# Two engines' orders in a slot loop: VectorE searches a tile's masked scores one slot earlier, and ScalarE counts the older tile first

## The chip, the cores and the metric

The kernel runs on one core of a Trainium2 chip. The metric is the device time of the whole program in microseconds (us): the median of three runs before the change is 3109.65 us (3107.92 to 3110.01). Another kernel's time is compared with it on the same chip.

## What is computed

The reference, cut to what matters. x has 16 sequences of 512 rows of 256 numbers; there are 16 heads of 16 numbers.

```python
Q, K, V = (x @ W.T + b, split in heads)
scores = einsum('bhqd,bhkd->bhqk', Q, K) / sqrt(D)          # 512 x 512 for each of 16 x 16 heads
thresh = top_k(scores, 31).values[..., -1:]                 # the 31st largest of each row
scores = where(scores < thresh, -inf, scores)
context = softmax(scores) @ V
x = layernorm(x + context @ Wo.T + bo)
h = silu(x @ wg.T) * (x @ wu.T)                             # int weights times 1/127, 768 wide
x = layernorm(x + h @ wd.T)
```

## The kernel before, in words

**Tiles and slots.** A tile is 128 rows of one head's 512 x 512 scores. A batch (one sequence) has 64 of them, and the program runs 64 slots for each of 16 batches, and a rest. Every engine has its own loop over the same slots (the five functions called `slots`), written out by hand. In slot n an engine does one step for tile n and one step each for older tiles; how much older is set by the lags of lines 48 to 61 (`COUNT0` = 1, `COUNT1` = 2, `BELOW` = 4, `BLOCK` = 5, `SORT` = 6, and so on). `due` says whether a lag's tile exists yet. Engines wait for one another by semaphores that count tiles. Nothing but these waits and the order in each loop sets the order of the work.

**The life of tile n.** The slot in which each step stands:

- slot n, TensorE, `scores`, L604: the tile's scores into one of two PSUM buffers `S_ps`. It waits for the evacuation of tile n-2.
- slot n, VectorE, `evacuate`, L870: copies them to `S` in SBUF with the rows' maxima. It comes after everything else that VectorE does in its slot for older tiles and for the bench (below), but for the residual sums and the flags' check.
- slot n+1, ScalarE, `count_first`, L469: how many scores of each row lie above an estimated threshold (a tanh with an accumulator); writes `s0`.
- slot n+2, ScalarE, `count_second`, L479: the same at a better threshold, from `s0`; it also writes the mask `above`.
- slot n+4, TensorE, `below`, L614, L615, L617: three matmuls build in one of two PSUM buffers `Y_ps` the scores that lie below the second threshold. They wait for the mask and for VectorE's search of tile n-2, which had the same buffer. `scores` of that slot follow right behind them. The rows of these two lie in other halves of the array, so L617 of one tile and L604 of another run at the same time.
- slot n+5, VectorE, `top_of_block`, L877: four MAX8, one for each block of 128 scores of `Y_ps`.
- slot n+6, VectorE, `sort_step`, L890, L893, L897: the 16 largest of the four blocks' 32 candidates. The three steps stand between the four MAX8 of a younger tile: step 0 ahead of the first.
- slots n+14 to n+17 by groups of 8 tiles, VectorE: `pick`, `pick_candidate` and `pick_threshold` at the head of a slot, and `check` at the end of one, which tells GpSimd of the thresholds (L964). A tile whose threshold can't be told in this way is sorted in full there (`general`, L940).
- slot n+17 and on, GpSimd, `cut`, L1109: the mask of what is under the threshold.
- slot n+23, TensorE, `turned`, L628, L631: the transposed scores again, masked, in the single PSUM buffer `ST_ps`. They wait for the exponentials of the tile before.
- slot n+24, ScalarE, `exponentials`, L487: exp of `ST_ps` into `PT`.
- slot n+25, TensorE, `values`, L645, for two tiles in every second slot.

**The bench.** Two further PSUM buffers, `bench`, serve all the rest (projections, statistics, context, feed-forward) at fixed slots (`HALF_USES`, `FFN_SLOTS` and the like, lines 74 to 84). TensorE fills one at the end of slot n, in `on_bench`, and the reader (VectorE or ScalarE) takes it in its slot n+1. A use waits until the use before last's buffer has been taken, and some wait for a result of the slot before: the matmul of L574 (slots 15 and 37) needs `gram`, which VectorE makes (L821) in the slot in which TensorE wants it; the flags of slot 48 (L660) need the buffer of the gate of slot 47, which VectorE takes (L1029) in slot 48.

**VectorE's slot**, in this order: the picks; then `sort_step` and `top_of_block` in turn; then what the bench holds for it; then `evacuate`; then residual sums, statistics and the flags' check.

**ScalarE's slot**, in this order: the exponentials; then what the bench holds for it; then `count_first`; then `count_second`; then, in four slots of a batch, the layer norms' last step (L492).

The lines that the change touches:

```python
BLOCK = 5
SORT = 6
...
                    if due(COUNT0, n, first, rest):
                        count_first(T, n, b, first)
                    if due(COUNT1, n, first, rest):
                        count_second(T, n, first)
```

Of the kernel before, what the change touches and what calls it, by code (L numbers as in the profile page):

```python
# [47 lines left out]
COUNT0 = 1  # L48
COUNT1 = 2
BELOW = 4  # L50
BLOCK = 5
SORT = 6
PICK = 14
PICKED = 15
THRESHOLD = 16
# [39 lines left out]
def due(lag, n, first, rest):  # L95
    return (n >= lag and not rest) or (n < lag and not first)
# [68 lines left out]
def build(nc, xT, x, wqT, wkT, wvT, woT, bq, bk, bv, bo, wgT, wuT, wdT, ident_in, blocks_in, heads_in, ranks_in, out):  # L165
    with ExitStack() as ctx:
# [242 lines left out]
        def _(act):  # L409
# [63 lines left out]
            def count_second(T, n, first):  # L473
                j = (n - COUNT1) % TILES
                hb, col = j // HALF_TILES, (j % NT) * HALF + j // NT % HALF
                act.wait_ge(cnt0_done, T - COUNT1 + 1)
                if not (first and n < COUNT1 + 4):
                    act.wait_ge(below_done, T - COUNT1 - 3)
                nc.scalar.activation(above[:, j % 4, :], S[:, score_place(j)[0], :], ACT.Sign, bias=s0[:, j % 8:j % 8 + 1],  # L479
                                     scale=steep[:, hb, col:col + 1], accum_out=s1[:, j % RING:j % RING + 1]).then_inc(cnt1_done, 1)  # L480
# [14 lines left out]
            def slots(b, first, rest, finish):  # L495
                for n in range(TILES):
                    T = b * TILES + n
                    uses = uses_of(n - 1, first, rest) if n else []
                    at = {use: place(b, n - 1, *use, first, rest) for use in uses}
                    if n % 16 == GROUP % 16 and due(GROUP, n, first, rest):  # L500
                        act.wait_ge(pv_done, T - PV)
                        nc.scalar.activation(ctxr[:, :], ctxT_ps[:, :], ACT.Copy).then_inc(raw_copied, 1)
                    if due(EXPO, n, first, rest):
                        exponentials(T, n, first)
                    for what, part in uses:
                        k, use = at[what, part]
                        if what in ("q", "k"):
                            split_high("qk".index(what), 1 if n < 32 else 0, (k, use), b + 1)
                        if what == "keys":
                            copy_keys((k, use))  # L510
                        if what == "v":
                            copy_values(VALUES_AT.index(n - 1), (k, use))
                        if what == "flags":
                            copy_flags(b, n, first, (k, use))
                        if what == "gate":
                            act.wait_ge(ready[k], use + 1)
                            if part:
                                act.wait_ge(h_done, (b - 1) * NF + part)
                            nc.scalar.activation(th[:, :], bench[k][:, :], ACT.Tanh, scale=0.5 * DEQ).then_inc(th_done, 1)
                        if what == "up":  # L520
                            act.wait_ge(ready[k], use + 1)
                            nc.scalar.activation(ups[:, :], bench[k][:, :], ACT.Copy, scale=0.5 * DEQ * DEQ).then_inc(taken[k], 1)
                        if what in ("ctx_t", "x1_t"):
                            act.wait_ge(ready[k], use + 1)
                            dst, done = (ctxT, taken[k]) if what == "ctx_t" else (x1T[0], x1T_copied)
                            nc.scalar.activation(dst[:, :, part * 2 * P:(part + 1) * 2 * P]
                                                 .rearrange("p c (n t) -> p n c t", n=2),
                                                 bench[k][:, :].rearrange("p (n c t) -> p n c t", n=2, c=C),
                                                 ACT.Copy).then_inc(done, 1)
                    if due(COUNT0, n, first, rest):  # L530
                        count_first(T, n, b, first)
                    if due(COUNT1, n, first, rest):
                        count_second(T, n, first)
                    if not first and n in X1_SLOTS:
                        normalised(b, 0, X1_SLOTS[n], x1_done)
                    if finish and n in OUT_SLOTS:
                        normalised(b - 1, 1, OUT_SLOTS[n], out_done)
# [260 lines left out]
        def _(dve):  # L798
# [74 lines left out]
            def top_of_block(T, n, i):  # L873
                j = (n - BLOCK) % TILES
                if i == 0:
                    wait_apart(dve, below_done, T - BLOCK + 1)
                mx = nc.vector.max(cand[:, j % CANDS, i, :], Y_ps[j % 2][:, i * BW:(i + 1) * BW])  # L877
# [118 lines left out]
            def slots(b, first, rest):  # L996
# [5 lines left out]
                for n in range(TILES):  # L1002
                    T = b * TILES + n
                    uses = uses_of(n - 1, first, rest) if n else []
                    at = {use: place(b, n - 1, *use, first, rest) for use in uses}
                    sorting, blocking = due(SORT, n, first, rest), due(BLOCK, n, first, rest)
                    if n % PAIR == PICK % PAIR and due(PICK, n, first, rest):
# [192 lines left out]
```

## Time and profile before

| | us |
|---|---|
| median of 3 runs | 3109.65 |
| the profiled execution | 3103.19 |
| its span | 3101.4 |
| granted TensorE clock, mean | 0.949 |
| TensorE busy | 2755.7 (89%) |
| VectorE busy | 2498.1 (81%) |
| ScalarE busy | 2498.3 (81%) |
| GpSimd busy | 2401.1 (77%) |

The profile is of one execution; its span is the time from the first to the last instruction. Engines are named PE (TensorE matmul), PEld (TensorE weight load), DVE (VectorE), ACT (ScalarE), POOL (GpSimd), SP (SyncE). L877 is line 877 of the kernel. Idle time of an engine is put down to what it last waited for, with an arrow: "<-DVE cand L877" means that VectorE's write of `cand` at line 877 ended the wait. All times in the timelines are from the span's start. In this trace the batch whose slot 0 has its L604 at 1680.27 us is batch 9 (counted from 0), the one before starts at 1499.5, and one at 1315.6.

### The profile page before, as it was taken

To read this page: it belongs to the slowest core of one execution; us is meant where nothing else is said; L and a number is where in the kernel's file an instruction comes from. 1 tells how busy PE (TensorE), PEld (TensorE's weight loads), DVE (VectorE), ACT (ScalarE), POOL (GpSimd) and SP (SyncE) were. 2 spreads that over 40 slices of the span, in tenths; PEclk is the share of its full clock that TensorE was granted. 3 is DMA by queue.
4 is the path that set the end of the run, shared out by engine and by line. 5 is a ranking of instruction groups with operands and counts; after the bars stand their busy time and mean duration, and the time that the engine had idled before them with its cause. 6 is when DMAs were issued, how large, how long until landed. Compare 5 with 4: busy or idle time off the path is not lost.

```text
span 3101.4 us, 81062 instructions
## 1 busy us (share of the span) xinstructions
PE 2755.7 (89%) x21030; PEld 1508.1 (49%) x21375; DVE 2498.1 (81%) x12298; ACT 2498.3 (81%) x5894; POOL 2401.1 (77%) x1677
## 2 busy tenths in 40 slices
PE   4988999999998998899999998999989998999986
PEld 2444544555454554544545454454545544454554
DVE  4888888888888878888888888878888888888861
ACT  4888888888888877788888888878878887888862
POOL 1887887788888876788788787877878787788882
PEclk7889999999999999999999999999999999999987
DMA  3201011120111101011010111102011020111000
GB/s 84 50 18 44 21 49 29 27 45 22 41 25 40 37 22 41 19 42 37 24 45 25 38 27 38 38 21 46 21 38 35 24 46 25 36 29 30 21 15 7
DMA packets 91143, 102.64 MB, mean 33 GB/s; under 512 B 34513, under 2 KB 52946, under 8 KB 90578
## 3 DMA queue, kind: packets, MB, share of 16 engines
q1 hardware_dynamic: 88544, 93.73, 12.7%
q8 instruction: 185, 3.03, 0.4%
q14 instruction: 380, 3.11, 0.3%
q10 hardware_dynamic: 2034, 2.76, 0.3%
HBM read 20.86 MB, written 8.39 MB: 9 GB/s over the span
## 4 chain that ended last, share of the span: by engine, by line
PE 53%; ACT 19%; issue 13%; DVE 11%; SPq 1%; POOL 1%; ACTq 1%; DVEq 1%; DMA 0%; POOLq 0%
ACT junk L469 8%; PE Y_ps L617 6%; PE ST_ps L628 6%; PE ST_ps L631 6%; PE ctxT_ps L645 6%; PE bench L681 6%; PE bench L687 6%; ACT above L479 4%; ACT PT L487 4%; PE Y_ps L615 4%; DVE cand L877 4%; PE bench L558 4%; PE Y_ps L614 3%; PE bench L674 2%; PE bench L589 2%
## 5 line engine op out<-in xcount | busy, mean ns | idle before, releaser
L1109 POOL TENSOR_SCALAR mask<-S,thr,mb 128x512 bf16<-128x512 f32 x1024 | 2113.6, 2076 | 43.0 <-POOL mb L1103 35.8
L877 DVE MAX8 cand<-Y_ps 128x8 f32<-128x128 f32 x4096 | 1069.7, 281 | 6.5 <-issue 6.4
L870 DVE TENSOR_SCALAR_CACHE_REDUCE S<-S_ps,na 128x512 f32<-128x512 f32 x1024 | 756.7, 739 | 320.4 <-PE S_ps L604 257.5
L469 ACT ACTIVATE junk<-S,at_zero,slope 128x512 bf16<-128x512 f32 x1024 | 827.1, 808 | 160.1 <-DVE S L870 155.6
L479 ACT ACTIVATE above<-S,s,steep 128x512 bf16<-128x512 f32 x1024 | 823.0, 804 | 0.0
L487 ACT ACTIVATE PT<-ST_ps 128x512 f32<-128x512 f32 x1024 | 596.0, 582 | 190.3 <-PE ST_ps L631 189.2
L628 PE MATMUL ST_ps<-QS,KS 64*128 64x512 f32 x1024 | 466.8, 456 | 130.0 <-ACT PT L487 126.9
L604 PE MATMUL S_ps<-KS,QS 64*128 64x512 f32 x1024 | 524.6, 513 | 4.2 <-DMA KS<-Klo 2.2
L617 PE MATMUL Y_ps<-KS,QS 64*128 64x512 f32 x1024 | 524.7, 512 | 1.2 <-issue 1.1
L615 PE MATMUL Y_ps<-above,nbig 128*128 128x512 bf16 x1020 | 400.1, 392 | 69.5 <-DVE cand L877 36.9
L631 PE MATMUL ST_ps<-nbig,mask 128*128 128x128 bf16 x4096 | 420.6, 227 | 0.0
L617 PEld LDWEIGHTS Y_ps<-KS,QS 64*128 64x128 f32 x1024 | 192.7, 188 | 458.0 <-issue 458.0
L1101 POOL TENSOR_SCALAR rbig<-rmax 128x8 f32<-128x8 f32 x128 | 31.1, 243 | 478.5 <-DVEq L964 478.5
L631 PEld LDWEIGHTS ST_ps<-nbig,mask 128*128 128x128 bf16 x4096 | 239.0, 100 | 319.6 <-issue 319.6
L645 PE MATMUL ctxT_ps<-PT,V 128*32 128x128 f32 x8192 | 349.8, 291 | 0.0
L614 PE MATMUL Y_ps<-ones_b,nbig 128*128 128x512 bf16 x683 | 273.7, 401 | 82.9 <-DVE cand L877 69.4
L628 PEld LDWEIGHTS ST_ps<-QS,KS 64*128 64x128 f32 x1024 | 196.8, 192 | 270.0 <-ACT PT L487 250.4
L645 PEld LDWEIGHTS ctxT_ps<-PT,V 128*32 128x32 f32 x8192 | 202.7, 113 | 58.8 <-issue 8.6
L890 DVE MAX8 best<-cand 128x8 f32<-128x32 f32 x1024 | 191.9, 187 | 40.0 <-issue 35.5
L614 PEld LDWEIGHTS Y_ps<-ones_b,nbig 128*128 128x128 bf16 x1024 | 100.5, 98 | 226.5 <-issue 169.7
L469 ACT ACTIVATION_READ_ACCUMULATOR junk<-S,at_zero,slope 128x1 f32 x1024 | 196.2, 192 | 0.0
L479 ACT ACTIVATION_READ_ACCUMULATOR above<-S,s,steep 128x1 f32 x1024 | 195.7, 191 | 0.0
(125 smaller groups left out, 3661.6 us busy)
## 6 DMA issues: line engine op xcount, KB each, us to landing
QS<-Qhi SPq DMA_DIRECT2D x512, 32.0 KB, 2.0
KS<-Khi SPq DMA_DIRECT2D x512, 32.0 KB, 2.0
KS<-Klo SPq DMA_DIRECT2D x512, 32.0 KB, 2.0
QS<-Qlo SPq DMA_DIRECT2D x512, 32.0 KB, 2.0
xTs<-in_xT SPq DMA_DIRECT2D x17, 512.0 KB, 3.7
xs<-in_x SPq DMA_DIRECT2D x16, 512.0 KB, 3.9
out<-xs SPq DMA_DIRECT2D x16, 512.0 KB, 2.9
hT<-in_wgT ACTq DMA_DIRECT2D x1, 768.0 KB
```

What stands on the lines that cost most here:

```text
L469: nc.scalar.activation(junk[:, :], S[:, score_place(j)[0], :], ACT.Tanh, bias=at_zero[:, :], scale=slope[:, hb, col:col + 1], accum_out=s0 ...
L479: nc.scalar.activation(above[:, j % 4, :], S[:, score_place(j)[0], :], ACT.Sign, bias=s0[:, j % 8:j % 8 + 1], scale=steep[:, hb, col:col + ...
L487: nc.scalar.activation(PT[:, j % 4, :], ST_ps[:, :], ACT.Exp, scale=SCALE).then_inc(exp_done, 1)
L604: nc.tensor.matmul(S_ps[n % 2][:, :], QS[rows, r, q:q + P], KS[rows, r, :], start=True, stop=True, tile_position=(rows.start, 0)).then_inc ...
L615: nc.tensor.matmul(Y[:, :], nbig[:, :], above[:, j % 4, :], start=False, stop=False)
L617: nc.tensor.matmul(Y[:, :], QS[rows, r, q:q + P], KS[rows, r, :], start=False, stop=True, tile_position=(rows.start, 0)).then_inc(below_do ...
L628: nc.tensor.matmul(ST_ps[:, :], KS[rows, r, kt * P:(kt + 1) * P], QS[rows, r, :], start=True, stop=False, tile_position=(rows.start, 0))
L631: mm = nc.tensor.matmul(ST_ps[:, t * P:(t + 1) * P], mask[:, h % MASKS, t, kt * P:(kt + 1) * P], nbig[:, :], start=False, stop=(t == NT - 1))
L645: mm = nc.tensor.matmul(ctxT_ps[32 * a:32 * a + 32, strip * P:(strip + 1) * P], V[:, k, grp, strip * VW:strip * VW + 32], PT[:, (j - kt + ...
L870: nc.vector.tensor_scalar(S[:, at, :], S_ps[n % 2][:, :], na[:, hb, col:col + 1], None, ALU.add, op1=ALU.max, accum_out=rmax[:, n % RING:n ...
L877: mx = nc.vector.max(cand[:, j % CANDS, i, :], Y_ps[j % 2][:, i * BW:(i + 1) * BW])
L1109: nc.gpsimd.tensor_scalar(mask[:, h % MASKS, t, :], S[:, score_place(j)[0], :], thr[:, r:r + 1], mb[:, r:r + 1], ALU.is_lt, op1=ALU.add).t ...
```

## The change

VectorE's search of a tile's masked scores stands in the slot in which TensorE writes them (lag 4, the lag of `BELOW`), no longer one slot on; the sort follows one slot behind the search, as before, so it is one slot earlier as well. In ScalarE's slot the second count (of tile n-2) stands ahead of the first count (of tile n-1). The instructions and their number stay the same, but for the first slots and the rest, where a lag begins or ends.

```diff
 COUNT0 = 1
 COUNT1 = 2
 BELOW = 4
-BLOCK = 5
-SORT = 6
+BLOCK = 4
+SORT = 5
...
+                    if due(COUNT1, n, first, rest):
+                        count_second(T, n, first)
                     if due(COUNT0, n, first, rest):
                         count_first(T, n, b, first)
-                    if due(COUNT1, n, first, rest):
-                        count_second(T, n, first)
```

Since `below` and `top_of_block` count by these lags, their waits move with them: `below` in slot n waits for the search that VectorE does in its slot n-2 (before: n-1), and `top_of_block` in slot n waits for `below` of TensorE's slot n (before: n-1).

## Rows read from the trace of the kernel before

**Rows 1.** The page's first part: busy time, share of the span, instructions

```profile
PE 2755.7 (89%) x21030; PEld 1508.1 (49%) x21375; DVE 2498.1 (81%) x12298; ACT 2498.3 (81%) x5894; POOL 2401.1 (77%) x1677
```

**Rows 2.** Who waited for whom: us in total, times, longest us

```profile
POOL rbig L1101 <- DVEq L964: 478.5, 112, 36.9
...
DVE S L870 <- PE S_ps L604: 257.5, 242, 4.2
...
ACT junk L469 <- DVE S L870: 155.6, 158, 9.4
PE ST_ps L628 <- ACT PT L487: 126.9, 246, 1.2
...
PE Y_ps L614 <- DVE cand L877: 69.4, 80, 6.9
...
PE Y_ps L615 <- DVE cand L877: 36.9, 36, 7.0
```

**Rows 3.** Timeline (start, us, engine, line, operation) of TensorE, slot 61 to 2

```profile
1671.87 0.49 PE L604 MATMUL S_ps<-KS,QS 64*128 64x512 f32 x1
...
1679.95 0.38 PE L615 MATMUL Y_ps<-above,nbig 128*128 128x512 bf16 x1 [0.86 <-DVE cand L877]
...
1680.82 0.50 PE L628 MATMUL ST_ps<-QS,KS 64*128 64x512 f32 x1
...
1685.10 0.50 PE L604 MATMUL S_ps<-KS,QS 64*128 64x512 f32 x1
1686.54 0.49 PE L628 MATMUL ST_ps<-QS,KS 64*128 64x512 f32 x1 [0.94 <-ACT PT L487]
```

**Rows 4.** Timeline of TensorE, slots 15 to 22 of an earlier batch

```profile
1357.17 0.50 PE L604 MATMUL S_ps<-KS,QS 64*128 64x512 f32 x1
...
1358.69 0.50 PE L574 MATMUL bench<-Qhi,gram 128*128 128x512 f32 x1 [0.17 <-DVE gram L821]
...
1374.20 0.59 PE L614 MATMUL Y_ps<-ones_b,nbig 128*128 128x512 bf16 x1 [1.25 <-DVE cand L877]
...
1375.14 0.79 PE L604 MATMUL S_ps<-KS,QS 64*128 64x512 f32 x1
```

**Rows 5.** Timeline of VectorE, evacuations of slot 61 and slot 0

```profile
1672.44 0.75 DVE L870 TENSOR_SCALAR_CACHE_REDUCE S<-S_ps,na 128x512 f32<-128x512 f32 x1 [1.11 <-PE S_ps L604]
...
1682.55 0.73 DVE L870 TENSOR_SCALAR_CACHE_REDUCE S<-S_ps,na 128x512 f32<-128x512 f32 x1
```

**Rows 6.** Timeline of VectorE in slot 17 of that earlier batch

```profile
1362.23 0.28 DVE L877 MAX8 cand<-Y_ps 128x8 f32<-128x128 f32 x1
...
1363.27 0.73 DVE L870 TENSOR_SCALAR_CACHE_REDUCE S<-S_ps,na 128x512 f32<-128x512 f32 x1
...
1363.93 0.19 DVE L890 MAX8 best<-cand 128x8 f32<-128x32 f32 x1
```

**Rows 7.** Timeline of ScalarE in slot 1 and the start of slot 2

```profile
1683.32 0.81 ACT L469 ACTIVATE junk<-S,at_zero,slope 128x512 bf16<-128x512 f32 x1 [0.43 <-DVE S L870]
...
1684.92 1.08 ACT L492 ACTIVATE xs<-xs,shift,rstd 128x256 f32<-128x256 f32 x2
1685.91 0.57 ACT L487 ACTIVATE PT<-ST_ps 128x512 f32<-128x512 f32 x1
```

**Rows 8.** Timeline of VectorE, the gram product of slot 15

```profile
1358.37 0.27 DVE L821 TENSOR_TENSOR gram<-bench,blk 128x128 fp32r<-128x128 f32 x1
```

**Rows 9.** Timeline of ScalarE, the first count in slot 21

```profile
1372.94 0.81 ACT L469 ACTIVATE junk<-S,at_zero,slope 128x512 bf16<-128x512 f32 x1 [0.86 <-DVE S L870]
```

**Rows 10.** Timeline of all engines, slots 48 to 50 of a later batch

```profile
1812.79 0.50 PE L604 MATMUL S_ps<-KS,QS 64*128 64x512 f32 x1
...
1812.84 0.66 DVE L1029 SCALAR_TENSOR_TENSOR th<-th,bench 128x512 f32<-128x512 f32 x1
...
1814.24 0.20 PE L660 MATMUL bench<-flag,onesc 128*1 128x9 f32 x2
...
1817.29 0.50 PE L628 MATMUL ST_ps<-QS,KS 64*128 64x512 f32 x1 [0.44 <-ACT PT L487]
```

## The prediction, made before the change was run

> **What bounds the kernel now.** I read the busy shares first [rows 1]: TensorE has 89%, and none of the others is far behind, 77 to 81%. So no engine is the bound everywhere, and the question is which wait ends last in each stretch. The list of waits [rows 2] shows a ring. VectorE waits for TensorE's scores (257.5 us), ScalarE's first count waits for VectorE's evacuation (155.6), and TensorE waits for ScalarE's exponentials (126.9) and for VectorE's search (69.4 + 36.9 = 106.3 us in 116 waits). The change aims at the last and, by its second part, at the 155.6. A gain of 106 us would be 3.4%; what I have to find out is how much of it stands on nothing else.
>
> So I followed the timelines of the three engines through the stretches where TensorE waits for the search. There are two in nearly every batch. One is at the batch's head, slots 0 to 2, with waits such as the 0.86 us in [rows 3]. The other is in slots 19 to 21, where VectorE computes the statistics of the next heads and never idles; its worst wait is 1.25 us [rows 4]. The rest is in a few long ones, up to 7.0 us [rows 2], where VectorE sorts a tile in full.
>
> **Part one, the search one slot earlier.** No instruction is added. Two waits move.
>
> (a) TensorE's `below` now needs the search of VectorE's slot n-2, not n-1. This takes most of the 106.3 us away from that wait. What is late next: `scores` in the same slot, right behind `below` on TensorE, needs the evacuation of tile n-2. And `turned`, behind both, needs the exponentials of ScalarE, which stand behind the first count, which needs the evacuation of tile n-1.
>
> (b) VectorE's first MAX8 now needs `below` of its own slot. Before, VectorE searched while TensorE was still at the bench work of the slot before, and then only waited for the scores, as 1.11 us in slot 61 [rows 5]. `below` and `scores` end together, so the search starts where the evacuation did: 1672.44 - 1671.87 = 0.57 us after L604's start [rows 3, 5]. From the first MAX8 to the evacuation are 1363.27 - 1362.23 = 1.04 us and from there to VectorE's next instruction 0.66 us [rows 6]. Wherever VectorE had waited for scores, its evacuation comes up to 1.04 us later. Queued behind the waiting MAX8 are sort steps 1 and 2, all bench takers of VectorE, the evacuation, the residual sums and the flags' check. Who waits for them: ScalarE's first count, TensorE's `scores` two slots on, GpSimd (L1101, after the check) and two bench uses that need VectorE in the same slot. I take these in turn.
>
> GpSimd: a check that ends 1.04 us later starts a group of eight masks as much later. GpSimd idles 478.5 / 112 = 4.3 us ahead of each group [rows 2], so it takes this up: nothing. No other DMA or queue is moved; SyncE's loads wait for steps far from these. If this cover were gone the price would be 1 us for each of 8 groups in a batch.
>
> **Part two, the second count first.** The second count needs a tile that was counted first a slot ago, so it never waits; it now fills up to 0.81 us (one ACTIVATE at L469 or L479, [rows 7]) of a wait for the evacuation. Between ends: at best 0.81 us for each of 158 waits = 128 us, at worst nothing, since the sum of ScalarE's work stays. Its price lies inside the stretches below.
>
> **The stretches, with both parts.**
>
> *Batch head.* VectorE had searched slot 61 ahead of the scores. Now that search starts at 1672.44, where the evacuation had started, and the evacuation follows 1.04 us later; with the residual sums, statistics and picks behind it VectorE has little idle time left until slot 2, so that its work is some 1.05 us later in slots 63 to 1. I worked the three queues through with durations from the trace. TensorE's 0.86 us wait at 1679.95 goes, but the next L628 needs an exponential that waited neither for this L604 nor for a search, so it stays at 1680.82 [rows 3]: the gain ends there. In slot 1 ScalarE is free at 1683.32 - 0.43 = 1682.89 [rows 7] and does the second count until 1683.7. The first count needs the evacuation of slot 0, which started at 1682.55 [rows 5], and now ends at 1682.55 + 0.66 + 1.05 = 1684.26; it starts at 1684.37 and ends 0.81 us later. The layer norm's step so starts at 1685.16 in place of 1684.92 [rows 7]: +0.24 us. From here to slot 4 ScalarE has no idle time and TensorE waits for it (0.94 us, [rows 3]), so the +0.24 stays. **+0.24 us a batch.**
>
> *Slots 13 to 24.* In slot 15 the gram product started at 1358.37 [rows 8], and L574, which waits for it, at 1358.69 [rows 4]. Now it can't start before 1357.17 + 0.57 + 1.04 = 1358.78, which is 0.41 us later; at most it is later by the whole 1.04. Nearer the upper end, since VectorE has already lost its head start in slots 12 and 13 and enters slot 14 late: I take 0.96, for L574 as well. This pushes slot 16 and with it VectorE's next search, so VectorE is, by my working, 1.4 us late in slots 18 to 22. In exchange TensorE's waits for the search in slots 19 to 21 are gone, and in ScalarE's slots (such as the 0.86 us of [rows 9]) the second count fills the wait. Working it through, the exponentials of slots 21 to 24 come at most 0.6 us later or 0.1 earlier than before, and L628 of slot 25 within -0.1 to +0.2. **I take +0.1 us.** What TensorE no longer waits for the search it waits for the exponentials.
>
> *Slot 48.* VectorE took the gate's buffer at 1812.84, almost with the scores. Now the take starts at 1812.79 + 0.57 + 1.04 = 1814.40 [rows 6, 10] and ends 0.66 later; the flags' matmul L660 starts at 1815.15, not 1814.24: 0.91 us. Of this 0.44 us is what TensorE waits for exponentials two slots on [rows 10], so **+0.46 us** stays. In slots 37 and 38 TensorE waits longer for ScalarE than the gram product of slot 37 could cost: nothing there.
>
> *Long sorts.* TensorE and ScalarE stand about one count (0.81 us, [rows 7]) further ahead in each of these; I found four in the timelines, 5 to 7 us long. **-3 us in all.**
>
> *Elsewhere* either TensorE is full (feed-forward, projections) and VectorE has several us in each long slot, or ScalarE is full and the later evacuation is still in time for the first count, which has itself moved 0.8 us on. I price those at nothing; the cover is ScalarE's own 0.8 us, and without it 1.04 - 0.81 = 0.23 us would be lost in a slot.
>
> **Sum.** (0.24 + 0.1 + 0.46) x 15 batches = 12, less 3: +9 us. On the profiled execution, 3103.2, this is 3112; that execution lies 6.5 us under the median, so for the median 3118.
>
> **Two rules of the Trainium skill.** The 1.25 us wait is followed by an L604 of 0.79 us where others take 0.50 [rows 4]: the clock has fallen from 2.4 towards 1.2 GHz there. "TensorE: Matmul & The Clock Gate" (HAM oscillation) says that idle gaps are what throttles the array; the trace agrees. As by my working the change swaps idle time for idle time of about the same sum, I leave the clock as it is. "Perfetto Trace Analysis" (Optimization Strategy) advises to find the gaps on the most-contended engine and make what ends them come sooner. By this alone the sum would be -106 us, which is my third rival; the rows say that the gap moves to the next instruction of the same queue.
>
> **The rivals.**
>
> - *The second count's filling pays (faster).* For it: in slots 17 to 21 of each batch ScalarE waits several times, up to 0.86 us [rows 9], and behind it TensorE. If VectorE is under 0.8 us late there, not 1.4, a wait of TensorE of 1.25 us [rows 4] and ScalarE's of 0.86 go without a substitute: -2.1, with +0.7 from head and slot 48, is -1.4 a batch, -21 us: 3088. It decides if VectorE's lateness at slot 18 stays below the 0.8 us of a count. Against it: L574 and the lost head start. 0.24.
> - *The same-slot hand-offs cost in full (slower).* L574 (0.96) and L660 (0.91) are not taken up by a later wait: 1.87 + 0.24 = 2.1 a batch, +31 us: 3141. It decides where TensorE reaches the next L628 after ScalarE has finished. 0.14.
> - *All waits for the search go:* 3004. 0.02.
> - *It does nothing:* one wait for another, in both directions, 3110 within 6 us. 0.18.
> - *My forecast,* +3 to +20 us, 3118: 0.42.
>
> **The numbers.** 0.2%, about what a measurement of this kernel can tell from no change, is 6.2 us. Faster: 0.24 + 0.02 = 0.26. Same: 0.18 and 0.08 of the forecast's lower edge, 0.26. Slower: 0.34 + 0.14 = 0.48. The range takes in the first and second rival's prices, as both signs hold much of the chance: 3086 to 3142; the forecast's own is 3112 to 3130.
>
> **What would show it.** PE's waits for DVE cand near 15 us or less; PE's waits for ACT PT up from 126.9 by 50 to 80 us; a new wait of DVE cand L877 for PE Y_ps of 200 us or more, and the one of S for S_ps nearly gone; L574 waiting near 1 us and L660 newly waiting for th. ACT junk's wait for S would fall to about half. If PE's waits for PT do not rise by about what those for cand fall, I am wrong on the faster side; if L574 and L660 wait as said and the time still falls, the slots that I priced at nothing held something.

## The result: slower by 2.5%, outside the range

| | before | after |
|---|---|---|
| median, us | 3108.78 | 3180.44 (3178.55 to 3198.73) |
| the profiled execution | 3103.19 | 3198.73 |
| its span | 3101.4 | 3196.9 |
| granted TensorE clock, mean | 0.949 | 0.928 |

The ratio is 1.0246 [1.0211, 1.028]. I had forecast 3118 us with a range up to 3142. The profiled execution of the changed kernel is 18.3 us above its own median, and its clock is the lowest of the runs (others about 0.935), so what is read from it overstates what the clock cost. I read it against the profiled execution of before: 95.5 us of span to explain. Span times granted clock splits it roughly (an estimate, and for the clock the upper one, since it counts idle time too): 0.949 x 3101.4 = 2943 and 0.928 x 3196.9 = 2967, so 24 us more at full clock and 72 us for the clock. For an execution near the median (3179.9 us at 0.934) it is 27 us and 51 for the clock. The clock is the larger part in both.

The changed kernel's busy time (first part of its page), beside [rows 1]:

```profile
PE 2839.4 (89%) x21030; PEld 1542.1 (48%) x21375; DVE 2508.7 (78%) x12298; ACT 2513.9 (79%) x5894; POOL 2403.9 (75%) x1677
```

With the same instructions, TensorE is busy 83.7 us longer and idle 357.5 us, where it was idle 345.7: the idle time grew by 11.8 us only. (Idle is the span less the busy time.) The waits of the changed kernel (engine, line, what for: us in total, times, longest us), beside [rows 2]:

```profile
POOL rbig L1101 <- DVEq L964: 560.8, 122, 37.2
...
DVE cand L877 <- PE Y_ps L617: 431.1, 386, 5.0
...
ACT junk L469 <- DVE S L870: 183.7, 183, 10.1
PE ST_ps L628 <- ACT PT L487: 171.9, 315, 1.9
...
ACT th L519 <- POOL hT L1146: 33.9, 47, 2.6
...
PE bench L574 <- DVE gram L821: 24.0, 19, 1.6
...
PE bench L660 <- DVE flag L928: 15.4, 13, 1.4
PE Y_ps L614 <- DVE cand L877: 15.2, 10, 4.8
PE bench L660 <- DVE th L1029: 13.4, 15, 1.7
...
PE Y_ps L615 <- DVE cand L877: 4.5, 1, 4.5
```

The waits moved much as forecast. TensorE's for the search are nearly gone (19.7 us after 106.3), L660 of slot 48 waits for `th`, and VectorE's new wait for the masked scores is 431 us. TensorE's waits for the exponentials rose by 45 us, a little less than the 50 to 80 forecast. Three lines were not forecast: ScalarE's first count waits longer, not half as long, the flags' matmul waits for `flag`, and ScalarE's tanh waits 33.9 us for GpSimd's product `hT`.

**Where the time went.** I took the start of every L604 from the trace and averaged the distances over batches 1 to 14 (my own reading, us per batch; the last row is the share of L604s in batches 1 to 15 that took over 0.6 us; they take 0.50 at full clock and 0.79 at the clock's lower level):

| slots | before | after | counts' order alone | search alone | evacuation first | takers first | evacuation first at the head | all in order |
|---|---|---|---|---|---|---|---|---|
| 63 to 0 | 2.57 | 1.84 | 2.56 | 1.81 | 1.90 | 1.81 | 1.86 | 1.85 |
| 0 to 5 | 16.30 | 18.45 | 15.57 | 18.06 | 16.32 | 17.58 | 16.31 | 16.62 |
| 5 to 15 | 25.69 | 25.51 | 25.67 | 26.09 | 25.74 | 25.61 | 25.63 | 25.62 |
| 15 to 26 | 26.94 | 29.41 | 27.10 | 30.90 | 27.84 | 28.41 | 30.74 | 27.92 |
| 26 to 46 | 60.90 | 60.68 | 60.81 | 63.47 | 60.49 | 60.55 | 60.49 | 60.26 |
| 46 to 53 | 20.68 | 21.94 | 20.70 | 22.13 | 21.99 | 21.16 | 21.82 | 22.07 |
| 53 to 63 | 33.28 | 34.42 | 33.76 | 34.32 | 33.21 | 33.90 | 33.66 | 33.37 |
| slow L604s | 0.041 | 0.080 | 0.045 | 0.098 | 0.050 | 0.068 | 0.071 | 0.045 |

(The last six columns are experiments, told below.) Four stretches carry the change: the head, slots 15 to 26, 46 to 53 and 53 to 63. In slots 26 to 46 nothing was lost, as forecast. Each column is one execution, and the same kernel's batches differ by the clock, so small differences between columns mean little.

**The head, batch 2.** TensorE's timeline before (start, us, what, in brackets the idle time before it), slots 0 to 2:

```profile
382.65 0.39 PE L614 MATMUL Y_ps<-ones_b,nbig 128*128 128x512 bf16 x1 [0.77 <-DVE cand L877]
...
384.55 0.38 PE L614 MATMUL Y_ps<-ones_b,nbig 128*128 128x512 bf16 x1 [0.30 <-DVE cand L877]
...
386.50 0.50 PE L628 MATMUL ST_ps<-QS,KS 64*128 64x512 f32 x1 [0.94 <-ACT PT L487]
```

and in the changed kernel, slots 0 to 3:

```profile
395.22 0.20 PE L660 MATMUL bench<-flag,onesc 128*1 128x9 f32 x2 [1.26 <-DVE flag L928]
395.40 0.39 PE L614 MATMUL Y_ps<-ones_b,nbig 128*128 128x512 bf16 x1
...
399.51 0.49 PE L628 MATMUL ST_ps<-QS,KS 64*128 64x512 f32 x1 [1.66 <-ACT PT L487]
...
401.47 0.79 PE L604 MATMUL S_ps<-KS,QS 64*128 64x512 f32 x1
```

The two waits for the search are gone. In front of the first now stands the flags' matmul of slot 0: its `flag` comes from the threshold step at the head of VectorE's slot 0 (L928), which stands behind slot 63's search and evacuation, now late. This is a third same-slot hand-off, and I had not seen it; what it costs is small, as experiment 9 shows. Then TensorE waits 0.72 us longer for the exponentials than before (1.66 against 0.94), and the next scores run at the lower clock.

**Slot 15, batch 7.** TensorE in the changed kernel:

```profile
1404.52 0.62 PE L574 MATMUL bench<-Qhi,gram 128*128 128x512 f32 x1 [1.34 <-DVE gram L821]
...
1405.95 0.79 PE L604 MATMUL S_ps<-KS,QS 64*128 64x512 f32 x1
...
1409.00 0.50 PE L604 MATMUL S_ps<-KS,QS 64*128 64x512 f32 x1
```

L574 starts 2.68 us after L604 of slot 15 in place of 1.52 [rows 4], 1.16 later, and so in nearly every batch. What follows runs at the lower clock for one slot, which takes 3.05 us (1405.95 to 1409.00) and took 2.12 us in the mean before.

**Idle or slow?** The windows view tells the two apart (from:to, length, busy time and instructions of PE, PEld, DVE, ACT, POOL, granted clock, DMA share, GB/s). Before, in this order: slots 0 to 5 of batch 2, 15 to 26 of batch 8, 46 to 53 of batch 9:

```profile
380.23:395.39 15.16, 11.86 (x112) 6.55 (x113) 11.55 (x64) 12.95 (x32) 12.00 (x9) 1.00 0.24 66
...
1539.63:1565.56 25.93, 22.66 (x196) 11.43 (x198) 24.85 (x138) 23.86 (x59) 21.24 (x17) 1.00 0.23 52
1807.23:1827.35 20.12, 18.94 (x152) 10.65 (x154) 16.85 (x82) 18.15 (x43) 19.67 (x14) 1.00 0.13 28
```

The changed kernel: slots 0 to 5 of batch 2; 15 to 26 of batches 2 and 8; 46 to 53 of batch 9:

```profile
392.15:411.74 19.59, 15.98 (x110) 9.11 (x112) 12.41 (x66) 13.78 (x33) 16.02 (x13) 0.74 0.17 56
...
436.52:463.21 26.69, 22.29 (x195) 11.34 (x197) 25.45 (x138) 24.26 (x59) 20.81 (x17) 1.00 0.23 51
...
1592.02:1624.52 32.50, 27.75 (x196) 13.64 (x198) 27.00 (x138) 25.01 (x60) 22.10 (x17) 0.79 0.23 51
...
1872.03:1893.38 21.35, 19.21 (x152) 10.51 (x155) 16.27 (x80) 18.96 (x44) 19.60 (x13) 1.00 0.13 29
```

The head of batch 2, one of the worst, is 4.43 us longer: 4.12 of it is busy time at a clock of 0.74, and 0.31 is idle (3.61 against 3.30). Slots 15 to 26 exist in two kinds. In four batches of 14 the clock stays at 1.00 and the stretch takes 26.7 us with all its new waits in it; in the other ten it takes 28.6 to 33.1 us, at a clock of 0.75 to 0.94, with nearly the same idle time (4.75 in batch 8, 4.40 in batch 2). The kernel before has both kinds too, and its mean of 26.94 holds some fallen clock: in two batches of 14 it keeps 1.00, and takes 25.9 us there (batch 8 above, 3.27 idle); the other twelve have 0.94. So at full clock the new waits cost 26.7 - 25.9 = 0.8 us, and the clock the other 1.7 of the mean's 2.47. Slots 46 to 53 keep their clock, and their 1.23 us are idle time for the most part (2.14 against 1.18).

Means over batches 1 to 14, read in the same way (idle, then busy, before -> after): head 3.10 -> 3.09 and 13.20 -> 15.35; slots 15 to 26 3.39 -> 4.47 and 23.56 -> 24.93; 46 to 53 1.51 -> 2.39 and 19.17 -> 19.56; 53 to 63 1.07 -> 1.05 and 32.21 -> 33.37. The head and the last stretch lost busy time only, and their mean clock fell from 0.88 to 0.76 and from 0.99 to 0.96.

### The profile page after: what moved, and what is told of

It reads as the page before. It is cut to its first block, busy times and chain, and to the rows that moved or that the text cites. A ratio compares the mean times of both kernels' runs of the same rounds, so it can differ in the third digit from the quotient of the medians.

```text
span 3196.9 us, 81061 instructions
## 1 busy us (share of the span) xinstructions
PE 2839.4 (89%) x21030; PEld 1542.1 (48%) x21375; DVE 2508.7 (78%) x12298; ACT 2513.9 (79%) x5894; POOL 2403.9 (75%) x1677
## 4 chain that ended last, share of the span: by engine, by line
PE 48%; ACT 16%; issue 16%; DVE 11%; POOL 5%; SPq 1%; DVEq 1%; ACTq 1%; DMA 0%; POOLq 0%
ACT above L479 6%; PE ST_ps L628 6%; PE ctxT_ps L645 6%; PE Y_ps L617 6%; PE ST_ps L631 5%; PE bench L687 4%; ACT junk L469 4%; POOL mask L1109 4%; PE bench L681 4%; DVE cand L877 4%; PE bench L558 4%; ACT PT L487 3%; PE Y_ps L615 3%; PE Y_ps L614 3%; PE bench L589 2%
## 5 line engine op out<-in xcount | busy, mean ns | idle before, releaser
L877 DVE MAX8 cand<-Y_ps 128x8 f32<-128x128 f32 x4096 | 1086.0, 286 | 438.4 <-PE Y_ps L617 431.1
L469 ACT ACTIVATE junk<-S,at_zero,slope 128x512 bf16<-128x512 f32 x1024 | 827.4, 808 | 184.3 <-DVE S L870 183.7
L628 PE MATMUL ST_ps<-QS,KS 64*128 64x512 f32 x1024 | 475.0, 464 | 176.4 <-ACT PT L487 171.9
L604 PE MATMUL S_ps<-KS,QS 64*128 64x512 f32 x1024 | 535.7, 523 | 6.0 <-DVE S L870 4.6
L617 PE MATMUL Y_ps<-KS,QS 64*128 64x512 f32 x1024 | 535.0, 523 | 1.0 <-issue 0.7
L615 PE MATMUL Y_ps<-above,nbig 128*128 128x512 bf16 x1020 | 408.8, 401 | 38.4 <-issue 19.3
L631 PE MATMUL ST_ps<-nbig,mask 128*128 128x128 bf16 x4096 | 428.8, 230 | 0.0
L645 PE MATMUL ctxT_ps<-PT,V 128*32 128x128 f32 x8192 | 357.5, 296 | 0.0
L628 PEld LDWEIGHTS ST_ps<-QS,KS 64*128 64x128 f32 x1024 | 202.0, 197 | 321.1 <-ACT PT L487 296.8
L614 PE MATMUL Y_ps<-ones_b,nbig 128*128 128x512 bf16 x683 | 280.7, 411 | 24.7 <-DVE cand L877 15.2
L604 PEld LDWEIGHTS S_ps<-KS,QS 64*128 64x128 f32 x1024 | 196.6, 192 | 11.5 <-DVE S L870 7.9
```

What stands on the lines that cost most here:

```text
L469: nc.scalar.activation(junk[:, :], S[:, score_place(j)[0], :], ACT.Tanh, bias=at_zero[:, :], scale=slope[:, hb, col:col + 1], accum_out=s0 ...
L604: nc.tensor.matmul(S_ps[n % 2][:, :], QS[rows, r, q:q + P], KS[rows, r, :], start=True, stop=True, tile_position=(rows.start, 0)).then_inc ...
L615: nc.tensor.matmul(Y[:, :], nbig[:, :], above[:, j % 4, :], start=False, stop=False)
L617: nc.tensor.matmul(Y[:, :], QS[rows, r, q:q + P], KS[rows, r, :], start=False, stop=True, tile_position=(rows.start, 0)).then_inc(below_do ...
L628: nc.tensor.matmul(ST_ps[:, :], KS[rows, r, kt * P:(kt + 1) * P], QS[rows, r, :], start=True, stop=False, tile_position=(rows.start, 0))
L631: mm = nc.tensor.matmul(ST_ps[:, t * P:(t + 1) * P], mask[:, h % MASKS, t, kt * P:(kt + 1) * P], nbig[:, :], start=False, stop=(t == NT - 1))
```

## Experiments

Theory H: with the search in its own slot, what VectorE hands over in the same slot comes about 1 us late, and the change loses by that and by the clock. Theory C: the loss is the order of ScalarE's counts. All times are medians; ratios are to the kernel before, run beside it on the same chip.

**1. The counts' order alone** (the kernel before, with the second hunk of the diff only).

```diff
+                    if due(COUNT1, n, first, rest):
+                        count_second(T, n, first)
                     if due(COUNT0, n, first, rest):
                         count_first(T, n, b, first)
-                    if due(COUNT1, n, first, rest):
-                        count_second(T, n, first)
```

> The kernel before with ScalarE's two counts in the changed order alone (the search stays at lag 5). Theory H (late hand-offs): all of the loss comes from VectorE's search, which now waits for TensorE's matmul of its own slot, makes evacuation and bench takers about 1.05 us late, and so lengthens single waits of TensorE (L628 of slot 0, L574 of slot 15, L660 of slots 0 and 48); the counts' order costs nothing and fills some waits: 3085 to 3110 us. Theory C (count order): the first count, which waits for the evacuation, now stands directly ahead of the next exponentials and the batch's change, and this costs: 3140 us or more.

Measured: 3092.57 us, 0.9945 [0.9928, 0.9962]: faster than both kernels. Its waits, beside [rows 2]:

```profile
DVE S L870 <- PE S_ps L604: 253.3, 232, 4.3
...
PE ST_ps L628 <- ACT PT L487: 116.1, 234, 1.2
PE Y_ps L614 <- DVE cand L877: 111.6, 116, 7.4
ACT junk L469 <- DVE S L870: 94.3, 96, 8.8
```

ScalarE's wait for the evacuation falls by 61 us, and TensorE's for the search rises by 42 us in L614: most of the gain is handed on. What is kept is in slots 0 to 5, where the undisturbed batches take 14.36 us and took 15.15: 0.79 us, about one count (0.81 us, [rows 7]). Over 15 batches that is 12 of the 17 us between the medians; where the other 5 lie I can't tell, since the two profiled executions differ by 3 us only (3099.85, the slowest of its four, and 3103.19).

**2. The search's slot alone** (the changed kernel with ScalarE's old order).

```diff
-                    if due(COUNT1, n, first, rest):
-                        count_second(T, n, first)
                     if due(COUNT0, n, first, rest):
                         count_first(T, n, b, first)
+                    if due(COUNT1, n, first, rest):
+                        count_second(T, n, first)
```

> The changed kernel with ScalarE's counts back in the old order (first count first); the search stays at lag 4. H: as slow as the changed kernel or slower, 3175 to 3230 us, since the first count now also loses its 0.8 us of slack. C: back near before, at most 3125 us.

Measured: 3278.09 us, 1.0568 [1.0518, 1.0617], clock 0.919. Two of its waits:

```profile
ACT junk L469 <- DVE S L870: 367.6, 462, 10.0
...
PE ST_ps L628 <- ACT PT L487: 228.7, 334, 2.5
```

ScalarE now waits for the late evacuation 462 times, 158 before. So the second part of the change covers much of the first part's damage: with it the time is 98 us lower. Theory C falls; the loss is the search's slot.

**3. Filler matmuls in the waits.** In the changed kernel, five matmuls without use ahead of L574 in slot 15, and seven ahead of L628 in slot 0. They give TensorE work while it would wait, and leave the waits' ends where they are.

```diff
+            def fill(k, times):
+                for _ in range(times):
+                    nc.tensor.matmul(bench[k][:, :], nbig[:, :], ones_b[:, :], start=True, stop=True)
...
                     pe.wait_ge(taken[k], use)
+                    if what == "quad" and n == 15:
+                        fill(k, 5)
...
+                    if n == 0 and not first and not rest:
+                        k, use = place(b, n, "flags", 0, first, rest)
+                        pe.wait_ge(taken[k], use)
+                        fill(k, 7)
                     if due(TURNED, n, first, rest):
```

> The changed kernel with idle TensorE time filled: 7 matmuls of no use (128x512 bf16, 0.22 us apart) into the free bench buffer ahead of L628 of slot 0 and 5 ahead of L574 of slot 15, in each batch. They lengthen no wait if the waits of 1.9 and 1.3 us stand there. If half of the loss is the fallen clock behind these waits (L604 at 0.79 us in slots 1, 3, 4, 16, 17): the low share of L604 falls from 8% to 5% or less, time falls by 20 to 40 us, to 3140 to 3160. If the clock has no part in it: within 5 us of 3180.

Measured: 3173.57 us, 1.0206 [1.0178, 1.0235], clock 0.941: not down to 3160, and the interval overlaps that of the changed kernel. Slots 15 to 26 fell to 27.88 us. The head rose to 18.88: I had put the filler before a matmul that waits long only in the one batch whose head falls on ScalarE's turn of its loop; elsewhere it delayed it. So I moved it.

**4. The filler ahead of the two hand-offs**, L574 in slot 15 and L660 in slot 0 (`if (what, n) in (("quad", 15), ("flags", 0)): fill(k, 5)`, and nothing at L628).

> The changed kernel with 5 idle matmuls (128x512 bf16, 1.1 us in all) in TensorE's wait ahead of L574 of slot 15 (1.3 us a batch) and 5 ahead of L660 of slot 0 (1.3 us), none ahead of L628. In e3_fill the 7 ahead of L628 of slot 0 lengthened that wait in most batches (it is 0.2 us there, 1.9 in one batch alone), while slots 15 to 25 fell from 29.4 to 27.9 us. If the clock behind the two hand-offs is what costs: slots 15 to 25 at 27.9 again, slots 0 to 4 down from 18.5 to 17.5, in all -2.5 us a batch, 3140 to 3150 us. If it is only the wait itself: 3178.

Measured: 3169.23 us, 1.0187 [1.0146, 1.0228], clock 0.943: lower than the changed kernel's 1.0246 [1.0211, 1.028], but the intervals overlap, and 3140 to 3150 was missed. Slots 15 to 26 take 27.78 us, 1.6 less than in the changed kernel, though they hold more matmuls. Its windows, batches 5 and 3:

```profile
992.53:1019.21 26.68, 23.83 (x204) 11.76 (x203) 25.45 (x138) 24.26 (x59) 20.84 (x17) 1.00 0.23 51
614.01:645.10 31.09, 28.01 (x204) 13.58 (x203) 26.53 (x138) 24.47 (x59) 22.04 (x17) 0.84 0.23 51
```

Seven of 14 batches are at 26.7 us now, four were. As one execution has few batches I counted those whose slots 15 to 26 keep a clock of 1.00 in all traces with L574 as late: 4 (changed kernel), 3 and 0 (experiments 7 and 9) without filler, 7 and 9 (experiments 3 and 4) with it. So the excess over 26.7 us is the clock, and TensorE's idle time at L574 has a part in its fall. The head did not gain (18.80): the idle time ahead of L660 is not what brings the clock down there.

**5. The evacuation ahead of the search, in all slots.**

```diff
-                    for i in range(BLOCKS):
-                        if sorting and i < 3:
-                            sort_step(T, n, i)
-                        if blocking:
-                            top_of_block(T, n, i)
...
                         evacuate(T, n, b, first)
+                    for i in range(BLOCKS):
+                        if sorting and i < 3:
+                            sort_step(T, n, i)
+                        if blocking:
+                            top_of_block(T, n, i)
```

> The changed kernel with VectorE's evacuation moved ahead of the search and sort of its slot (behind the bench takers): order is picks, bench takers, evacuation, search and sort. H: evacuation and bench takers are back at the time that they had before or earlier, the search waits for nothing; L574 and L660 wait no longer, TensorE's waits for the search stay away: 3070 to 3105 us. C: the order of counts still costs, 3140 us or more.

Measured: 3129.22 us, 1.0073 [1.0052, 1.0095], clock 0.947. That takes away 51 of the 72 us, but misses the forecast 3070 to 3105. The clock is nearly that of before, the head is at 16.32 us again. Left over: slot 0 (+0.56 us a batch against before), slots 19 and 20 (+0.71 and +0.47) and 47 (+1.34).

**6. The same-slot takers ahead of the search**, the evacuation behind it as in the change: the gram products (slots 15 and 37) and the gate's last part (slot 48).

```diff
+                    early = [u for u in uses if u[0] == "gram" or u == ("gate", 2)]
+                    for what, part in early:
+                        k, use = at[what, part]
+                        if what == "gram":
+                            head_gram((k, use))
...
                     for i in range(BLOCKS):
```

> The changed kernel with VectorE's two bench takers that TensorE wants in the same slot (gram of slots 15 and 37, gate of slot 48) ahead of the search. If these hand-offs are the cause in their stretches: L574's wait of 24 us and L660's for th of 13 us go, slots 15 to 25 fall from 29.4 to about 27.3 us, slots 46 to 52 from 21.9 to about 21.0, in all -3 us a batch: 3130 to 3145 us. If VectorE's lateness itself (evacuations) is the cause: less than 10 us of gain.

Measured: 3149.99 us, 1.0137 [1.009, 1.0184], clock 0.937. L574 starts 1.55 us after its slot's L604 again, L660 of slot 48 1.44 us. Slots 15 to 26 gain 1.0, 46 to 53 gain 0.8 us a batch. This is at the upper end of what was expected; the head gained too (17.58), which I had not expected.

**7. GpSimd's product `hT` ahead of its slot's mask.** GpSimd waits 82 us longer for the flags' check than before, and ScalarE's wait for `hT` was all but new (8.0 us before).

```diff
-                    if due(MASK, n, first, rest):
-                        cut(b, T, n, first)
                     for what, part in uses_of(n - 1, first, rest) if n else []:
...
+                    if due(MASK, n, first, rest):
+                        cut(b, T, n, first)
```

> The changed kernel with GpSimd's feed-forward product (L1146) ahead of its slot's mask. In the changed kernel the check, and with it the masks of the group of slots 41 to 48, came some 1 us later, and the product behind them kept ScalarE's tanh of slot 46 waiting (0.75 us). If GpSimd's lateness costs: slots 46 to 52 fall from 21.9 by 0.4 to 0.8 us, -6 to -12 us in all: 3168 to 3174. If GpSimd has slack: 3180, or slower through later masks.

Measured: 3189.55 us, 1.0252 [1.0218, 1.0287]: no gain. Slot 47 is back at 3.46 us (3.94 in the changed kernel), so its loss was `hT`; but slot 48 went from 3.21 to 3.66 us, and the stretch stayed at 21.84.

**8. Takers first, `hT` first, and the evacuation first in slots 60 to 63 and 0 to 4.** The diffs of 6 and 7, and that of 5 under the condition `n >= 60 or n < 5`.

> The changed kernel with e6 and e7 and with the evacuation ahead of the search in slots 60 to 63 and 0 to 4 (in e4, which did so everywhere, slots 63 to 4 took 18.2 us, before 18.9, changed 20.3). If the loss is the sum of these places (head 2.1, slots 15 to 25 2.3, slots 46 to 52 1.2 us a batch): 3095 to 3120 us, at or a little over before. If something else costs through all slots: over 3130.

Measured: 3132.01 us, 1.007 [1.0035, 1.0105], clock 0.942. The head is at 16.08 us, slots 46 to 53 at 21.15; slots 15 to 26 take 26.3 us in seven batches with the clock up, less than in the changed kernel. It misses 3095 to 3120; something else costs too.

**9. The evacuation first in slots 60 to 63 and 0 to 4, nothing else.**

> The changed kernel with VectorE's evacuation ahead of its search in slots 60 to 4 alone; all other slots as changed. If the batch's head is lost by the evacuation's lateness, slots 0 to 5 fall from 18.45 us to near 16.1 us, as in the run where it stood beside two other edits, and this alone brings some 2.2 x 15 = 33 us: near 3147. If the two other edits had a part in it, slots 0 to 5 stay above 17 us and the time above 3160. Slots 15 to 26 stay near 29 us, since the gram product of slot 15 is still behind the search.

Measured: 3171.59 us, 1.0177 [1.0156, 1.0198]. The head fell to 16.31 us as expected, by 2.14 us a batch (32 us in 15 batches). The total fell by less than the 33 us expected: 9 us between the medians, 0.69 points or 21 us by the two ratios. L660 of slot 0 starts as late as in the changed kernel (3.02 and 2.98 us after L604 in the mean), so the wait for `flag` has at most the 0.5 us that the head is still above before at full clock. Windows of slots 0 to 5 of batch 9 and 15 to 26 of batch 8:

```profile
1722.71:1738.35 15.64, 12.28 (x110) 6.55 (x112) 12.56 (x67) 13.48 (x33) 11.92 (x11) 1.00 0.22 63
1572.21:1604.09 31.88, 27.91 (x196) 13.45 (x198) 26.56 (x138) 24.48 (x59) 22.78 (x18) 0.79 0.23 51
```

The head runs at full clock and costs 0.5 us more than before. But slots 15 to 26 have a fallen clock in all 14 batches of this execution, 29.1 to 32.0 us, with the same wait at L574. Whether the repair of the head brought that about is not shown: with the same repair experiment 8 keeps the clock up in seven. And the single repairs do add up by their ratios: experiments 6, 7 and 9 gain 1.09, -0.06 and 0.69 points on the changed kernel, 1.72 in all, and experiment 8, which has all three, gains 1.76.

**10. Everything in order**: evacuation first in all slots and the takers first, that is 5 and 6 together.

> The changed kernel with every same-slot hand-off of VectorE ahead of its search: the evacuation in all slots, the gram products and the gate's last part. The search keeps its earlier slot, the sort too, and ScalarE's second count is first. If late hand-offs are the whole of the loss, what is left is the gain of the count order and of the search's earlier slot: 3092 as with the count order alone, or less by what the waits for the search (69 + 37 us) are worth. If something else of the earlier slot costs (the search now ends late for the next slot's below, the flags' check of slot 0 comes late), it stays above the kernel before, near 3115 to 3125, with waits for cand near 90 us in slots 18 to 21.

Measured: 3130.22 us, 1.005 [1.0033, 1.0067], clock 0.949. The first branch of the expectation (3092) failed; the second (3115 to 3125) is 5 us too low. With evacuation and takers ahead of the search and the clock of before, the earlier search still loses against experiment 1. What stays behind the search is the slot's tail: residual sums, statistics and the flags' check. Its waits:

```profile
DVE S L870 <- PE S_ps L604: 249.1, 248, 4.5
...
PE ST_ps L628 <- ACT PT L487: 141.2, 259, 1.4
...
PE Y_ps L614 <- DVE cand L877: 69.0, 58, 5.6
...
PE Y_ps L615 <- DVE cand L877: 24.5, 17, 6.8
```

TensorE's waits for the search are back, 93.5 us against 106.3 in [rows 2]. The code says why: VectorE's queue is now evacuation of slot n, search, the slot's tail, next slot's picks, takers, evacuation, and before it was evacuation, tail, picks, search, takers, evacuation. With the evacuation first, the earlier slot moves the search over the tail and the picks only, and makes these a search later. The tail holds the flags' check (L964) for which GpSimd waits, and the picks hold the threshold step for the flags of slot 0 (wait for L928: 20.1 us, 0.2 before).

The profiled execution has the clock of before, and its 27.0 us of longer span are idle time (374.9 against 345.7 us, busy 2753.5 against 2755.7). The largest piece is slot 47, 4.93 us in place of 3.46 in the mean. Batch 9, before: GpSimd starts the mask group 11.39 us ahead of L604 of slot 46 (1807.23) and has `hT` ready at 1806.23, ahead of that slot:

```profile
1795.84 0.24 POOL L1101 TENSOR_SCALAR rbig<-rmax 128x8 f32<-128x8 f32 x1 [3.27 <-DVEq L964]
...
1804.94 1.29 POOL L1146 TENSOR_TENSOR hT<-th,ups 128x512 f32<-128x512 f32 x1
```

With everything in order, engine by engine:

```profile
1815.72 0.24 POOL L1117 TENSOR_SCALAR rbig<-rmax 128x8 f32<-128x8 f32 x1 [3.49 <-DVEq L964]
...
1824.84 1.28 POOL L1162 TENSOR_TENSOR hT<-th,ups 128x512 f32<-128x512 f32 x1
```

```profile
1826.15 0.60 ACT L519 ACTIVATE th<-bench 128x512 f32<-128x512 f32 x1 [1.70 <-POOL hT L1162]
```

```profile
1825.56 0.49 PE L604 MATMUL S_ps<-KS,QS 64*128 64x512 f32 x1
...
1829.45 0.46 PE L628 MATMUL ST_ps<-QS,KS 64*128 64x512 f32 x1 [1.29 <-ACT PT L487]
```

The check comes behind the search, so the group starts 9.84 us ahead of L604 of slot 46, 1.55 us later than before. The product stands behind the group's first masks in GpSimd's queue and is late with them, ScalarE's tanh waits 1.70 us for it, the exponentials stand behind the tanh, and TensorE waits 1.29 us for them. Over 15 batches this slot makes 22 us. Moving the product ahead of the masks, which cured slot 47 in experiments 7 and 8, was not tried together with this order.

## Why the prediction was wrong

The direction was right, and most of the waits came out as forecast. These steps failed:

- **"As by my working the change swaps idle time for idle time of about the same sum, I leave the clock as it is."** This is the step that cost most. The premise was right, and closer than it deserved: TensorE's idle time rose by 11.8 us, and my sum was +9. The conclusion was wrong: busy time rose by 83.7 us. L604's mean went from 513 to 523 ns; that alone would be some 54 us on 2755.7 (2%, an estimate). TensorE is busy at the lower clock level for 404.4 us, before for 250.4; if that work is stretched as L604 is (0.50 to 0.79 us), the 154 us more hold 57 us of the 83.7, and 77 if everything takes twice as long (an estimate as well). The rest I can't divide, since matmuls that run side by side less often also count as longer busy time. The rule that I cited, of the Trainium skill, "TensorE: Matmul & The Clock Gate" (HAM oscillation), that idle gaps throttle the array, agrees with experiments 3 and 4, where work in the gap kept the clock up more often. I had read the fall after the 1.25 us wait in [rows 4] and did not ask where the new waits, as long, would stand.
- **Slots 13 to 24, "I take +0.1 us".** Too low even without the clock: like against like, at full clock, slots 15 to 26 take 26.7 us against 25.9, +0.8, and L574 came 1.16 us later, not 0.96. Most of that delay was not taken up by the waits for the search that went. Ten batches of 14 lost 2 to 6 us to the clock on top, where twelve had lost about 1 us before. So the mean was +2.47.
- **"Batch head. +0.24 us a batch."** Measured +2.15, less 0.73 in slot 63. The idle time of slots 0 to 5 did not grow at all in the mean (3.10 and 3.09 us): the whole is busy time at a fallen clock. Two things were missed. I followed ScalarE's first count and the layer norm, and overlooked that VectorE's threshold step at the head of slot 0 makes the `flag` for which L660 of slot 0 waits: 1.26 us in batch 2. In [rows 3] no wait stood there, and TensorE waited for the search right behind it, so nothing pointed to it but the code. That one is small: experiment 9 keeps it and has the head back at 16.31 us. And the clock fell. What experiment 9 takes away is the long wait of L628 in slot 2 for the exponentials (up to 1.77 us in the changed kernel, 0.63 at most there, 0.94 before), so I take this to be the wait behind which it fell; no run isolates it. With the evacuation first, the head at full clock costs only 0.5 us more than before.
- **"Slot 48. +0.46 us stays."** L660 came 1.07 us later (2.52 against 1.45 after L604), and slots 46 to 53 lost 1.26 us in the mean. The order of size was right, but little was absorbed. 0.48 of it is slot 47, which I had at nothing; experiment 7 shows that this piece is GpSimd's `hT`.
- **"Between ends"** for the second count's filling: what it gives on its own is 17 us (3092.57 against 3109.7), some 12 of them in the head; together with the early search, where ScalarE would wait far more often, 98 us. "ACT junk's wait for S would fall to about half": it rose from 155.6 to 183.7, since there the evacuation was up to 1 us later and the filling of 0.8 us did not cover it. Experiment 1 shows the fall of 39% that the second part alone gives.
- **GpSimd, "takes this up: nothing".** The 82 us that it waits longer say little, since its work stayed (2401.1 and 2403.9 us busy) while the program grew by 95.5. What failed is the path: I looked at GpSimd's idle time ahead of the masks, and not at the product `hT` that stands behind them and that ScalarE waits for. It costs 0.48 us a batch in slot 47 of the changed kernel, though experiment 7 won no time by curing it, and 1.47 us with everything in order (experiment 10).
- **Long sorts, -3 us.** The longest of these waits fell from 7.0 us [rows 2] to 4.8. The four stretches with a long sort (batch 6 slots 31 to 39 and 46 to 53, batch 12 slots 7 to 15, batch 14 slots 0 to 8) were 6.3, 7.9, 9.8 and 8.3 us longer than the median of the other batches, and are 7.4, 8.5, 8.4 and 6.2 us longer now: 1.6 us less in all, right in sign and half the size, but with both signs among the four.

What the rivals said: the one on the slower side, hand-offs that cost in full, named L574 and L660 as the place and gave 3141. It was the nearest, 39 us short, mostly for the clock. "All waits for the search go" describes the waits and not the time: some 87 us of 106 went and the kernel is slower.

**What stays open.** What decides in which batches the clock falls: experiments 5 and 10 have as long a wait in slot 47 (1.3 us) and the clock stays up there in 13 and 12 batches of 14, while after L574 it falls in most batches. The 53 to 63 stretch (+1.14 us), where L604s of slots 57 and 58 run slow, is the clock too: batches that keep 1.00 take about 33.3 us against 33.1, but the clock is below 1.00 in 7 of 14 batches and was in 2; why it falls there I have not found. And why the earlier search loses another 38 us against experiment 1 in experiment 10: slot 47 has 22 of them, slots 19 and 20 (+0.64 and +0.40 us a batch against before) and slot 0 (+0.51) come next, partly offset elsewhere, and no run cures them.

## What to carry to other kernels

An engine that waits for fresh data should have work on older data ahead of that wait in its queue: moving VectorE's search to its own slot took such a filler away, moving ScalarE's second count forward made one, and the second alone gave 0.55%. Before a step is put ahead of others on an engine, list every result that the engine hands over in the slot in which it is made, also those made at a slot's head, which inherit the lateness of the slot before, and ask what stands behind each result in its reader's queue: GpSimd's masks had time to spare, the product behind them had not. And when a change leaves TensorE's idle sum alone but places the waits anew, read the granted clock behind each wait of that length; the same idle sum was followed by 84 us more of busy time here.

## What the runs showed of the hardware

- The same stretch of instructions with nearly the same idle time took 26.7 or 32.5 us in one execution, at granted clocks of 1.00 and 0.79. L604 takes 0.50 us at 2.4 GHz and 0.79 us at the lower level.
- Matmuls without use in a wait of TensorE can hold the clock up: slots 15 to 26 kept 1.00 in 7 and 9 of 14 batches with five fillers ahead of L574 (experiments 3 and 4), in 4, 3 and 0 without (the changed kernel, experiments 7 and 9). That the whole program gained by it is not clear of noise (ratios 1.0206 and 1.0187 against 1.0246, intervals that overlap).
- Idle time alone does not tell what a stretch costs: the head's was 3.1 us before and after, and it took 2.15 us longer, at a mean clock of 0.76 and not 0.88.
